# Gate and up projections with 4-bit weights: one scale group multiplied without its scale, the bank scaled in place

## The reference

```
w_gu = values(gate_up_packed) * scale[group of 128 inputs, output]   # 2816 x 512, four scale groups
gate, up = split(x @ w_gu.T)                                         # 1408 each = 11 tiles of 128
h = silu(gate) * up
y = h @ (values(down_packed) * scales).T
out = layernorm(x + y / rms(y))
```

## Time and profile before

| what | us |
|---|---|
| median of three runs (lowest, highest) | 800.64 (799.73, 802.24) |
| the profiled execution, its own time | 798.36 |
| its span, first to last instruction | 796.6 |
| TensorE busy | 725.3 (91%) |
| VectorE busy | 472.4 (59%) |
| ScalarE busy | 358.0 (45%) |
| GpSimd busy | 200.7 (25%) |

### The profile page before, as it was taken

The page is one execution under the profiler, slowest core; times in us unless marked ns, Lnnn a source line. Parts: engine busy times, 40 slices in busy tenths (PEclk is TensorE's granted clock), DMA queues, the critical chain, the costliest instruction groups (busy, mean ns, idle before and its releaser), DMA issues.

```text
span 796.6 us, 11725 instructions
## 1 busy us (share of the span) xinstructions
PE 725.3 (91%) x4662; PEld 584.0 (73%) x4662; DVE 472.4 (59%) x918; ACT 358.0 (45%) x572; POOL 200.7 (25%) x235
## 2 busy tenths in 40 slices
PE   4899998999999898579899999999999999999993
PEld 3688777877787786357777777777777777788883
DVE  4568668764677767766736458655568464632314
ACT  5345453357353733563524472545353635531214
POOL 0454344354453559711201000211000111000000
PEclk9999999999999998669999999999999999999998
DMA  9500101002300320130001130030130030100201
GB/s 329 186 16 3 51 2 41 15 1 71 116 14 1 102 72 2 53 106 1 2 26 53 53 106 0 1 133 1 53 106 1 10 122 1 53 0 1 106 0 54
DMA packets 25408, 41.18 MB, mean 52 GB/s; under 512 B 5002, under 2 KB 7690, under 8 KB 25226
## 3 DMA queue, kind: packets, MB, share of 16 engines
q1 hardware_dynamic: 23194, 37.40, 13.9%
q10 hardware_dynamic: 2160, 3.02, 1.1%
HBM read 28.88 MB, written 11.53 MB: 51 GB/s over the span
## 4 chain that ended last, share of the span: by engine, by line
PE 61%; DVE 23%; ACT 9%; DMA 2%; issue 2%; POOL 1%; ACTq 0%; DVEq 0%; POOLq 0%
PE ps L1645 22%; PE ps L1659 12%; PE ps L1281 10%; PE ps L1365 3%; DVE small L413 3%; PE ps L1320 2%; PE ps L525 2%; PE ps L534 2%; DMA rms_col<-in_L_attn_rms_w_dram 2%; DVE masked L1200 2%; DVE act_s L406 1%; PE ps L1348 1%; DVE w L406 1%; DVE weights L738 1%; ACT w L276 1%
## 5 line engine op out<-in xcount | busy, mean ns | idle before, releaser
L1645 PE MATMUL ps<-x2T_hi,weights 128*128 128x512 f32 x704 | 217.4, 390 | 0.0
L1645 PEld LDWEIGHTS ps<-x2T_hi,weights 128*128 128x128 f32 x704 | 132.3, 188 | 26.8
L1645 PE MATMUL ps<-x2T_lo,weights 128*128 128x512 f32 x352 | 141.6, 402 | 0.9 <-DVE x2T_lo L1544 0.9
L1659 PE MATMUL ps<-weights,h_hi 128*128 128x512 f32 x352 | 110.8, 396 | 1.8 <-DVE h_lo L1538 1.8
L1554 DVE TENSOR_TENSOR silu<-ps,silu 128x512 f32<-128x512 f32 x44 | 30.3, 689 | 134.1 <-PE ps L1645 127.1
L1281 PE MATMUL ps<-wqkv_lo,xT_hi 128*128 128x512 f32 x192 | 80.9, 421 | 9.8 <-DVE wqkv_lo L1149 5.8
L1468 ACT ACTIVATE silu<-ps 128x512 f32<-128x512 f32 x44 | 26.2, 596 | 114.9 <-PE ps L1645 114.9
L1645 PEld LDWEIGHTS ps<-x2T_lo,weights 128*128 128x128 f32 x352 | 66.2, 188 | 14.7 <-DVE x2T_lo L1544 1.2
L1659 PEld LDWEIGHTS ps<-weights,h_hi 128*128 128x128 f32 x352 | 64.8, 188 | 15.5 <-DVE h_lo L1538 2.5
L1281 PE MATMUL ps<-wqkv_hi,xT_lo 128*128 128x512 f32 x192 | 76.0, 396 | 0.0
L1281 PE MATMUL ps<-wqkv_hi,xT_hi 128*128 128x512 f32 x192 | 75.9, 395 | 0.0
(11 more groups left out here) (181 smaller groups left out, 1381.0 us busy)
## 6 DMA issues: line engine op xcount, KB each, us to landing
w<-in_fside_BxS2xS_dram SPq DMA_DIRECT2D x4, 1024.0 KB, 5.2
x_dram<-xb SPq DMA_DIRECT2D x4, 1024.0 KB, 4.3
xc<-x_dram SPq DMA_DIRECT2D x4, 1024.0 KB, 5.5
x_in<-in_x_dram SPq DMA_DIRECT2D x15, 256.0 KB, 3.4
xb<-x_dram SPq DMA_DIRECT2D x3, 1024.0 KB, 5.5
out_dram<-xc SPq DMA_DIRECT2D x3, 1024.0 KB, 4.8
z<-in_x_dram SPq DMA_DIRECT2D x3, 768.0 KB, 4.9
x_dram<-z SPq DMA_DIRECT2D x3, 768.0 KB, 3.5
```

What stands on the lines that cost most here:

```text
L1645: last = nc.tensor.matmul(dst[:, :], lhs, rhs, start=(k == 0 and n == 0), stop=(k == NK - 1 and n == 2))
L1659: last = nc.tensor.matmul(ps[c][:, :], lhs, rhs, start=(it == 0 and n == 0), stop=(it == NI - 1 and n == 2))
```

## The change

For k = 0 the piece is no longer scaled: its product uses an identity instead of a diagonal, it holds bare 4-bit values, which need no low part, and no diagonal is made for it. TensorE multiplies it in two passes (values x low part of the input, values x high part) into the empty bank; then VectorE multiplies bank 4 (gate) and ScalarE bank 5 (up) in place by the column of scales of group 0; then the other three groups, nine passes, are added on the scaled bank. The two unscaled passes of the next tile's gate are issued behind up and place 3it+1, those of its up after the second of four chunks of the down product (for tile 1 at once). VectorE's scaling stands between the product and the low part, ScalarE's behind the high part. For a batch's first tile they stand within the last down product of the batch before, VectorE's scaling within the input split, ScalarE's between the input split and the squares.

```diff
+        def scale_up(b, it):
+            act.wait_ge(up_unscaled, b * NI + it + 1)
+            nc.scalar.activation(ps[5][:, :], ps[5][:, :], ACT.Copy, scale=weights.unscaled_scale(1, it))\
+                .then_inc(up_scaled, 1)
...
             nc.scalar.activation(silu[:, it % 2, :], ps[4][:, :], ACT.Silu).then_inc(silu_done, 1)
             beside(3 * it)
             hidden_hi(b, it)
+            if it + 1 < NI:
+                scale_up(b, it + 1)
             beside(3 * it + 1)
             beside(3 * it + 2)
...
             split_x2T(b)
+            if b == 0:
+                act.wait_ge(weights.unscaled_cols_set, 1)
+            scale_up(b, 0)
             if b > 0:
                 squares(b - 1)
...
+        def scale_gate(b, it):
+            dve.wait_ge(gate_unscaled, b * NI + it + 1)
+            nc.vector.tensor_scalar(ps[4][:, :], ps[4][:, :], weights.unscaled_scale(0, it), None, ALU.mult)\
+                .then_inc(gate_scaled, 1)
...
                 .then_inc(h_done, 1)
+            if it + 1 < NI:
+                scale_gate(b, it + 1)
             hidden_lo(b, it)
...
+        def unscaled(b, it, half, dst, filled):
+            pe.wait_ge(x2T_lo_done, b * NK + half + 1)
+            ...
+            nc.tensor.matmul(dst[:, :], values, x2T_lo[:, UNSCALED, :], start=True, stop=False, skip_group_check=True)
+            nc.tensor.matmul(dst[:, :], values, x2T_hi[:, UNSCALED, :], start=False, stop=True, skip_group_check=True)\
+                .then_inc(filled, 1)
+
+        def unscaled_gate(b, it):
+            if it > 0:
+                pe.wait_ge(silu_done, b * NI + it)
+            unscaled(b, it, 0, ps[4], gate_unscaled)
+
+        def unscaled_up(b, it):
+            if it > 0:
+                pe.wait_ge(h_done, b * NI + it)
+            unscaled(b, it, 1, ps[5], up_unscaled)
+
         def hidden(b, it, half, dst):
-            for k in range(NK):
+            pe.wait_ge(up_scaled if half else gate_scaled, b * NI + it + 1)
+            for k in range(1, NK):
...
         def inner_tile(b, it, beside):
-            if it > 0:
-                pe.wait_ge(silu_done, b * NI + it)
+
+            def next_unscaled(c):
+                if c == 1 and it + 1 < NI:
+                    unscaled_up(b, it + 1)
+
             hidden(b, it, 0, ps[4]).then_inc(gate_ps, 1)
             beside(3 * it)
-            if it > 0:
-                pe.wait_ge(h_done, b * NI + it)
             hidden(b, it, 1, ps[5]).then_inc(up_ps, 1)
             beside(3 * it + 1)
-            if it == 1:
-                pe.wait_ge(f_z, b * NC + 1)
-            if it > 0:
-                down(b, it - 1)
+            if it + 1 < NI:
+                unscaled_gate(b, it + 1)
+            if it == 0:
+                unscaled_up(b, it + 1)
+            else:
+                if it == 1:
+                    pe.wait_ge(f_z, b * NC + 1)
+                down(b, it - 1, next_unscaled)
             beside(3 * it + 2)
```

More of the change, by code:

```diff
@@ L145, in gate_up @@
             pieces.append(("gate_up", pair, k, len(tiles), at))
-            at += 4 * len(tiles) * P
+            at += (2 if k == UNSCALED else 4) * len(tiles) * P
     def down(it):
@@ L178 @@
 DIAGS, MORE_DIAGS = 4, 6
-DIAG_OF = [m % (DIAGS + MORE_DIAGS) if m < FIRST_BESIDE else (m - FIRST_BESIDE) % DIAGS for m in range(len(PIECES))]
+SCALED = [m for m, piece in enumerate(PIECES) if piece[0] == "down" or piece[2] != UNSCALED]
+SCALED_IN_ROW = sum(m < FIRST_BESIDE for m in SCALED)
+DIAG_OF = {m: n % (DIAGS + MORE_DIAGS) if n < SCALED_IN_ROW else (n - SCALED_IN_ROW) % DIAGS
+           for n, m in enumerate(SCALED)}
 def expert_order():
@@ L664, in use, with scaled, scaled_to @@
         return self.ps[bank], self.expert.full[bank - 6], self.expert.drained[bank - 6], EXPERT_USE["piece", m]
+    def scaled(self, m):
+        return m in DIAG_OF
+    def scaled_to(self, m):
+        return sum(n <= m for n in SCALED)
     def count(self, m):
@@ L673, in parts @@
         at, width = PIECES[m][4], self.count(m) * P
-        return self.tiles[:, at:at + width], self.tiles[:, at + width:at + 2 * width]
+        return [self.tiles[:, at + n * width:at + (n + 1) * width] for n in range(2 if self.scaled(m) else 1)]
     def gate_up(self, k, up, it):
@@ L689, in diagonals @@
         kind, where, k, tiles, _ = PIECES[m]
-        before = [n for n in range(m) if DIAG_OF[n] == DIAG_OF[m]]
+        before = [n for n in SCALED if n < m and DIAG_OF[n] == DIAG_OF[m]]
         if before:
@@ L714, in product @@
         for n in range(self.count(m)):
+            by = self.diags[DIAG_OF[m]][:, n, :] if self.scaled(m) else self.ident16[:, :]
             if kind == "gate_up":
@@ L720, in product @@
                 values = self.values_dn[:, n * I + where * P:n * I + (where + 1) * P]
[L721 to L722 removed]
+            last = self.nc.tensor.matmul(bank[:, n * P:(n + 1) * P], values, by, start=True, stop=True)
         last.then_inc(full, 1)
     def hi(self, act, m):
[L727 removed]
+        bank, full, drained, at = self.use(m)
         act.wait_ge(full, at + 1)
@@ L1525, in pool_program, with next_diagonals @@
         steps = expert.pool_steps(pool)
+        def next_diagonals(m):
+            n = weights.scaled_to(m) - 1 + DIAGS
+            if weights.scaled(m) and n < len(SCALED):
+                weights.diagonals(pool, SCALED[n])
         for b in range(B - 1):
-            beside = place(steps, {}, b, lambda m: weights.diagonals(pool, m + DIAGS) if m + DIAGS < len(PIECES) else None)
+            beside = place(steps, {}, b, next_diagonals)
             for at in range(3 * NI):
@@ L1662, in down @@
                     last.then_inc(y_ps, 1)
-            if it < NI - 1:
-                last.then_inc(down_read, 1)
+                if c == NC - 1 and it < NI - 1:
+                    last.then_inc(down_read, 1)
+                after_chunk(c)
         def transpose_x2(b):
```

65 lines of the change are left out of this document (47 added, 18 removed).

## The result

| | before | after |
|---|---|---|
| median, us (lowest to highest) | 801.44 (799.73 to 802.24, 4 runs) | 812.58 (810.0 to 816.46, 4 runs) |
| ratio, 95% interval | | 1.0152 (1.011 to 1.0193) |
| the profiled execution, span | 798.36, 796.6 | 812.29, 810.5 |

The kernel became slower by 11.1 us in the medians and by 13.9 us in the profiled executions. The forecast was 811.5.

A forecast was written before the change was run, and what follows sets the result against it. In expert batches a VectorE, ScalarE and short-transpose chain bounds some 40 of 113 us, in batch 3 TensorE alone. Terms +2.1, +13.0 and -3.6 sum to +11.5 us, giving 811.5 us, range 798 to 819.

The forecast's parts named there:

- batch 0 with the pieces: Pieces before the stage -1.0, tiles 0 to 2 -0.4, later tiles +2.7, batch end +0.8: +2.1 us.
- batch 1: Feed-forward batch with expert work: +3.0, +2.7 and +0.8 make +6.5 us, the same for batch 2.
- batch 3: Batch without expert work: first tiles +0.5, then 9 tiles at -0.453 each: -3.6 us.
- tiles 0 to 2: Start of batch 1: squares, table load and silu queue behind scale_up(0), TensorE waits for tile 1's product: +3.0 us.
- tiles 2 to 9: Middle of batch 1: row transposes, xq and wq drains and aq1 come late behind the scalings: +2.7 us.
- end of the batch: Second y products stand behind 4 unscaled passes, so VectorE's rescale and the chain to normalisation come late: +0.8 us.
- the clock of the stage falls under 0.98: Sign in the changed profile that the forecast is wrong: clock of the feed-forward stage under 0.98 for the new gaps.
- The scaling in the bank: VectorE's scaling of the gate bank, taken as 0.68 us and mostly hidden; only a batch's first tile sees it.
- A: Rival: TensorE keeps its bound, product there within 1.8 us of up in every tile: 780 to 794 us, 10%.
- B: Rival: a draw, expert batches lose only what hangs on their first tiles: 799 to 805 us, 16%.
- D: Rival: only the batch start hurts, tiles 2 to 9 come out even: 803 to 806 us, 12%.
- C: Rival: ScalarE's queue costs more, scale_up delaying xq, wq, v rounding and aq by 3 to 4 us: 816 to 823, 12%.

The follow-up runs named there:

- Experiments 1: Kernel before with the third pass of group 0 left out of gate and up, order unchanged: 787.36 us, ratio 0.9831.
- experiment 2: Changed kernel's bare pieces and two passes, but the old order and waits and no scalings: 784.9 us, ratio 0.9798.
- experiment 6: Changed kernel with the unscaled up pair behind all four chunks of the down product, not two: 836.49 us, ratio 1.0448.
- 4: Changed kernel with the squares ahead of ScalarE's scaling of a batch's first tile: 813.81 us, ratio 1.0155.
- Experiments 5: Changed kernel with scale_up of the next tile behind the work of places 3it+1 and 3it+2: 811.62 us, ratio 1.0139.
- 7: Changed kernel with squares first, scale_up behind both places' work and unscaled up behind the whole down product: 807.3 us, ratio 1.0086.
- 8: Changed kernel with unscaled up inside its own tile's gate, scale_up right ahead of silu, squares first: 807.03 us, ratio 1.009.
- the last: Kernel of experiment 9 plus unscaled gate of tile 1 inside up of tile 0, its scaling ahead of product 0: 795.95 us, ratio 0.9965.
- experiment 9: Kernel of 8 with scale_up(4) moved between round_x and round_w on ScalarE in batches 0 to 2: 796.76 us, ratio 0.9964.
- experiment 3: Changed kernel without the two scalings and their waits, unscaled passes at their new places: 798.46 us, ratio 0.9971.

## Why the prediction came out

**The total** was right: 811.5 forecast, 812.58 measured. On the profiled execution the sum was +11.5 and the measurement +13.9 us, so it is 2.4 us short there; the medians are 11.1 apart. Part of the agreement is luck: the measured terms hold falls of the clock that the sum has no term for, and the term for tiles 2 to 9 was too high by 0.6 us a batch, which hid some of them.

| step (us) | forecast | measured |
|---|---|---|
| batch 0 with the pieces | +2.1 | +3.4 |
| batch 1 | +6.5 | +6.8 |
| batch 2 | +6.5 | +6.6 |
| batch 3 | -3.6 | -3.2 |
| in batch 1: tiles 0 to 2 | +3.0 | +3.8 |
| tiles 2 to 9 | +2.7 | +2.1 |
| end of the batch | +0.8 | +0.9 |

**Batch 0** is the term furthest off. The transposes at 348.52 start at 346.99, 1.5 us earlier (forecast 1.0); that this comes from the pieces is not shown, since kernels with the same pieces start them from 344.8 to 350.2. The half clock, which had ended at 351.7, lasted until 354.9, and by the product of tile 2 only 0.3 of the forecast 1.4 us was left. The prediction did not ask what an earlier start meets. The fall at 389.05 lies in the same batch.

**The start of a batch.** The chain was the one forecast: squares behind scale_up(0), table load, silu 2.3 us behind its gate, product of tile 1, TensorE waiting. It is 0.8 us longer because the unscaled up of tile 0 ends 4.0 us behind the start of the down product, not 3.25, and those passes ran at the lower clock. Batch 3 of the same kernel, which starts in the same order and without a fall, has its first product 8.83 us behind the start of the down product; batches 1 and 2 have it at 9.72 and 9.51, so the fall costs 0.9 and 0.7 us. Without it tiles 0 to 2 of batch 1 would be at +2.9, beside +3.0 forecast. Here "at full clock" was taken over from before without a word. The sign "the clock of the stage falls under 0.98" was not met over the whole stage (0.98, 1.00 before), but batch 0 alone is at 0.95.

**The scaling in the bank** was sized 0.68 and took 0.755 us. TensorE waits under 0.5 us in all for it. The Trainium skill, "VectorE: DVE Perf Modes", section "Why PSUM operands drop a tier", says an fp32 operand in a bank runs at the plain rate. The trace agrees in direction: 755 ns in a bank, 542 from SBUF. ScalarE's was also sized 0.68 and took 0.660, so the sum moves by under 0.3 us. The rule of the Trainium skill, "ScalarE: Activation LUTs", section "Step-by-step: what each stage is for", that a bank is the quicker destination fits only in part: 660 is under the 681 with a column as bias into SBUF, and over the 603 of the plain copy there.

**Tiles 2 to 9.** The waits named were there at about the sizes named, but for one: TensorE was to wait for the drains of xq and start gate of tile 5 2.2 us late, and it doesn't wait for them at all. Counted from the product of tile 2, the product of tile 6 comes 1.0 us late (forecast 1.35), that of tile 7 0.5 (0.9) and that of tile 9 2.1 (2.7), so most of the 0.6 us is there by tile 6. The step was thus sized too high, and partly for a wait that isn't there.

**Batch 3** gave 0.453 us per tile from tile 2 on, with no idle time: the one part of the argument that is arithmetic alone.

**The rivals.** A, TensorE keeps its bound, is out in this order: the unscaled pass waits for the product in tiles 1 and 3 as the arithmetic of VectorE's queue said. Experiments 1 and 2 show its world, at 787 and 785. B and D are out, as batches 1 and 2 cost 6.6 to 6.8. C, ScalarE's queue costing more, is out for the change, but it is what happens in experiment 6, where two chunks later make 24 us, three more falls of the clock among them. The order was close to that edge.

**Where my own follow-ups failed.** Five expectations in a row (4 to 8) and the last missed. Experiments 5 to 8 share one reason: I priced the wait that an edit removes and not the queue into which it puts the instruction. In 5, 7 and 8 scale_up(4) got behind round_x and round_w; in 6 scale_up, with the drains of xq and wq already behind it, had to wait longer. None of these four counted the falls of the clock either. Only when the idle time of ScalarE was read line by line around that one place did an edit do what it should.

## What to carry to other kernels

An operation put between two matmul groups on the same bank cost twice here: the first group stands earlier and waits there for the bank's last reader (13.6 us with all that follows from the new place), and the operation stands in some engine's queue (14 us). Price both before the passes saved: for each new wait list what stands behind it on that engine, and for each moved instruction what stands in front of it. An engine idle for half of the time is no cover; look for the gap in its own timeline in which the instruction fits, since one such gap in three batches was worth 10 us here, the clock that came back with it included.

## What was not expected of the hardware

- TensorE fell to half clock within a stage in which it was busy for nine tenths of the time: 3.41 us each at 389.05, 467.55 and 587.02, the second 1.7 us behind a wait of 1.58 us. The busy share of a batch doesn't tell whether the clock holds: batch 1 of experiment 9 (104.0 of 113.3 us, 92%) stayed at 1.00, and batch 1 of experiment 2 (104.5 of 110.8 us, 94%) fell for 3.41 us at 503.90. Nor do the waits alone: batches 1 and 2 of experiment 3 have the same ones up to the fall at 597.32, which only batch 2 has. What brings a fall was not isolated. One cost 1.6 us there.
- `tensor_scalar` of 128x512 fp32 with a column of scales, in place in a bank, takes 755 ns on VectorE, more than a subtraction with one operand in the bank (680). The same on ScalarE takes 660 ns.
